# Four attention layers and a feed-forward on one core: last layer's weights kept as three values, smaller start loads, new instruction order

## The reference, cut to what matters

```
L0    post-norm cross attention, key mask        y = LN(x + Att(x, ctx) Wo + bo)
L1    the same, no mask                          y = LN(x + ...)
L2    pre-norm block: causal self attention (SELF), cross attention (CROSS), feed-forward 256-1024-256 (FFN)
L3    pre-norm cross attention with quantised weights:
      def bit_quant(W):
          gamma = mean(|W|)
          return clip(round(W / (gamma + 1e-5)), -1, 1) * gamma
      xn = layer_norm(x, ln_gamma, ln_beta)
      q = xn @ bit_quant(Wq).T + bq ;  k = ctx @ bit_quant(Wk).T + bk ;  v = ctx @ bit_quant(Wv).T + bv
      out = x + softmax(q k^T / 4) v @ bit_quant(Wo).T + bo
```

## Time and profile before

| | us |
|---|---|
| median of 3 runs | 1303.33 |
| the profiled execution, its own time | 1301.78 |
| its span, first to last instruction | 1299.9 |
| TensorE busy (union of matmuls) | 1240.0 |
| VectorE busy | 1065.7 |
| ScalarE busy | 793.9 |
| GpSimd busy | 706.1 |

### The profile page before, as it was taken

How to read it: one execution, slowest core, us unless ns; L and a number is a source line. 1 busy time by engine, 2 the same in 40 slices (tenths; PEclk the granted TensorE clock), 3 DMA queues, 4 the chain that set the end, 5 groups by cost and what they waited for, 6 DMA issues and landing times.

```text
span 1299.9 us, 42570 instructions
## 1 busy us (share of the span) xinstructions
PE 1240.0 (95%) x18540; PEld 1016.2 (78%) x18540; DVE 1065.7 (82%) x1826; ACT 793.9 (61%) x1263; POOL 706.1 (54%) x847
## 2 busy tenths in 40 slices
PE   7999999999999999999999999999999999899997
PEld 6777777777777788888888777777898989677775
DVE  6799998999999888798878999998544446888986
ACT  5666777757765676656658677666332424666654
POOL 5453667756885576364445246327856668324411
PEclk9999999999999999999999999999999999999999
DMA  6411101010110010000000001001010000001002
GB/s 240 126 38 30 45 10 34 9 34 17 28 31 3 2 34 11 3 2 3 2 3 3 12 16 34 25 19 38 5 33 1 1 1 2 9 10 34 26 3 99
DMA packets 16594, 34.89 MB, mean 27 GB/s; under 512 B 2071, under 2 KB 7447, under 8 KB 15895
## 3 DMA queue, kind: packets, MB, share of 16 engines
q1 hardware_dynamic: 16407, 32.16, 7.9%
HBM read 27.96 MB, written 4.19 MB: 25 GB/s over the span
## 4 chain that ended last, share of the span: by engine, by line
PE 55%; DVE 22%; POOL 10%; ACT 6%; issue 5%; DMA 2%; SPq 0%; POOLq 0%; DVEq 0%; ACTq 0%
DVE s_nm L1482 9%; PE ps L1111 7%; PE ps L996 6%; PE ps L1167 6%; PE ps L1179 5%; PE ps L1194 5%; PE ps L1148 5%; PE ps L1049 4%; PE ps L1008 3%; PE ps L1021 3%; ACT s_PU L1339 3%; DVE s_Os L1489 2%; DVE s_KH L1439 2%; PE ps L1126 2%; PE ps L1145 2%
## 5 line engine op out<-in xcount | busy, mean ns | idle before, releaser
L1482 DVE TENSOR_REDUCE s_nm<-ps 128x8 fp32r<-128x960 f32 (+1 forms) x352 | 398.1, 1160 | 40.2 <-PE ps L1049 19.0
L1339 ACT ACTIVATE s_PU<-ps 120x1024 f32<-120x1024 f32 (+1 forms) x288 | 281.9, 1023 | 110.6 <-PE ps L1126 109.6
L1667 POOL TENSOR_TENSOR s_Os<-s_Os,s_Rc 128x512 f32<-128x512 f32 x80 | 86.9, 1087 | 307.5 <-DVE s_Rc L1497 304.3
L1111 PE MATMUL ps<-s_Qs,s_KH 32*120 32x256 f32 (+2 forms) x4608 | 192.3, 289 | 13.3 <-DVE s_nm L1482 3.1
L1111 PEld LDWEIGHTS ps<-s_Qs,s_KH 32*120 32x120 f32 (+1 forms) x4608 | 154.6, 180 | 45.5 <-issue 13.0
L1167 PE MATMUL ps<-s_W,s_oT 128*128 128x256 f32 x960 | 134.5, 290 | 7.1 <-DVE s_oT L1411 6.2
L1148 PE MATMUL ps<-s_PU,s_Vp 120*32 120x256 f32 x2048 | 135.5, 388 | 4.2 <-DVE s_nm L1482 1.2
L996 PE MATMUL ps<-s_xT,s_W 128*128 128x256 f32 (+1 forms) x768 | 134.8, 324 | 3.3 <-DVE s_W L1416 1.0
L1167 PEld LDWEIGHTS ps<-s_W,s_oT 128*128 128x128 f32 x960 | 120.7, 191 | 16.4 <-issue 8.2
L1614 POOL TENSOR_TENSOR s_xs<-s_xs,s_rowv 128x512 f32<-128x512 f32 x96 | 125.2, 1304 | 11.4 <-POOL s_mv L1652 1.1
L1049 PE MATMUL ps<-s_KH,s_Qs 32*128 32x240 f32 x3072 | 126.9, 291 | 4.6 <-DVE s_nm L1482 2.4
(11 more groups left out here) (93 smaller groups left out, 2303.4 us busy)
## 6 DMA issues: line engine op xcount, KB each, us to landing
s_cf<-ctx_t SPq DMA_DIRECT2D x32, 240.0 KB, 2.7
s_ws<-weights SPq DMA_DIRECT2D x28, 256.0 KB, 2.9
s_nt<-x_t SPq DMA_DIRECT2D x16, 256.0 KB, 3.5
s_xs<-x_nat SPq DMA_DIRECT2D x4, 1024.0 KB, 7.5
out<-s_xs SPq DMA_DIRECT2D x16, 256.0 KB, 2.6
s_rowv<-rows SPq DMA_DIRECT2D x6, 512.0 KB, 3.8
s_mi<-mask SPq DMA_DIRECT2D x8, 120.0 KB, 4.2
s_who<-who SPq DMA_DIRECT2D x1, 128.0 KB, 3.5
```

Of the source, the lines that this page charges most:

```text
L1111: t = e.matmul(banks[j][0:n, wide * x:wide * x + wide], kz[row[j], lk, g, c, k0:k0 + n], q[row[j], lq, g, qs_], start=(x == 0 and y_ == 0) ...
L1339: t = e.activation(P_of(i, k)[0:n, :, :], pair("B", i, k)[0:n, :, :], ACT.Exp, scale=0.25)
L1482: e.tensor_reduce(o, v, AX.X, ALU.max, negate=True).then_inc(sem["max"])
L1667: e.tensor_tensor(o[:, :, 0:16], o[:, :, 0:16], rc.to_broadcast([128, 32, 16]), ALU.mult).then_inc(sem["pool"])
```

## The change

1. In L3 the weights hold -1, 0 and 1, which fp32r holds exactly, so the part with the rest of the weight falls away: `parts_of("L3")` is `PARTS[:2]`, 4 matmuls to an output tile in place of 6, in Q, K, V and O. The means are applied elsewhere: into x^T with the norm's scale (Th, Tl), and into the copies of K (K0), V (Ve) and O (y).
2. The making of these weights: qa keeps only its three small operations; qw is now two DVE operations of 128x512 straight into the weight's place, which wait until that place has been read last. Wh, Wl and wg of L3 are gone, and POOL's three operations.
3. Start: the constants are loaded sixth, `who` and `gone` much later (before SELF), the mask row goes to 4 partitions (the rest of the tile is set once by two memsets on DVE), x comes in eight loads of 512 KB.
4. The due times of all steps on all engines are new, and so are the planner's durations. By the two tables TensorE's list has 1213 steps in both, and changes between whole-array, row-tiled and column-tiled steps 660 times before and 661 times after.

```diff
+TERNARY = ("L3",)
-MOVED = dict(xT=.65, cT=.6, mi=.8, ws=.65, row=1.5, x=2.7, mci=.5, out=.65)
+MOVED = dict(xT=.65, cT=.6, mi=.15, ws=.65, row=1.5, x=1.35, msk=.6, cst=.4, mci=.4, out=.65)
-TURN = .19
+TURN = {("whole", "rows"): .195, ("columns", "rows"): .3, ("rows", "whole"): .185, ("columns", "whole"): .2,
+        ("whole", "columns"): .03, ("rows", "columns"): .03}
+def ready_of(layer, m):
+    return ("qw", m, 0) if layer in TERNARY else (rest_of(layer), layer, m)
+def parts_of(layer):
+    return PARTS[:2] if layer in TERNARY else PARTS
...
+        def mean_of(m): return gq[:, 4 * m + 1:4 * m + 2]
...   (in Q, K, V and O alike)
-                    for c, (cw, cx) in enumerate(PARTS):
+                    for c, (cw, cx) in enumerate(parts_of(layer)):
...   (Th on ACT, Tl on DVE)
+                    if layer_of(i) in TERNARY:
+                        w.wait_ge(sem["wa"], nth("wa", layer_of(i), 0))
+                        e.activation(to, half_of("T", i, f), ACT.Copy, scale=gg[:, f:f + 1]).then_inc(sem["Th"])
+                    e.scalar_tensor_tensor(xT_of(i)[:, 1, at, :], half_of("T", i, f), gg[:, f:f + 1], xT_of(i)[:, 0, at, :].bitcast(f32),
+                                           ALU.mult, ALU.subtract).then_inc(sem["Tl"])
...   (wa, K0, Ve, y)
+                    e.tensor_scalar(gg[:, :], c2[:, 20:22], mean_of(0), None, ALU.mult)
+                        t = e.activation(K0_of(i)[:, g, :], m[:, g * 256:g * 256 + n], ACT.Identity, bias=bk(layer_of(i), g), scale=mean_of(1))
+                        t = e.scalar_tensor_tensor(to, v, mean_of(2)[0:n], add, ALU.mult, ALU.add)
+                    e.scalar_tensor_tensor(to, bankM(name, i), mean_of(3), to, ALU.mult, ALU.add).then_inc(sem["y"])
...   (qa on DVE loses its last two operations, POOL loses qw; new on DVE:)
-                e.tensor_scalar(a1, w3(m), c[2], c[1], ALU.is_gt, ALU.mult)
-                e.tensor_scalar(b1, w3(m), c[3], c[1], ALU.is_lt, ALU.mult).then_inc(sem["qa"])
+            def qw(m):
+                over, under = (gq[:, 4 * m + k:4 * m + k + 1] for k in (2, 3))
+                to, low = (wv("L3", c, m).rearrange("p k n -> p (k n)") for c in range(2))
+                last = readers(*had_place("L3", m))
+                w.wait_ge(sem["qa"], 2 * nth("qa", m))
+                w.wait_ge(sem[last[0][0]], max(nth(*x) for x in last))
+                e.tensor_scalar(low, w3(m), under, None, ALU.is_lt).then_inc(sem["q1"])
+                w.wait_ge(sem["q1"], nth("qw", m))
+                e.scalar_tensor_tensor(to, w3(m), over, low.bitcast(f32), ALU.is_gt, ALU.subtract).then_inc(sem["qw"])
...   (start)
+                e.memset(mi[s][:, :], 1).then_inc(sem["cst"])
-            e.dma_start(cst[:, :], consts).then_inc(sem["d_cst"], 16)
-                e.dma_start(xs[:, 4 * n:4 * n + 4, :, :], x_nat[:, 4 * n:4 * n + 4, :, :]).then_inc(sem[f"d_x{n}"], 16)
+                e.dma_start(xs[:, 2 * n:2 * n + 2, :, :], x_nat[:, 2 * n:2 * n + 2, :, :]).then_inc(sem[f"d_x{n}"], 16)
-                e.dma_start(mi[slot("mi", i)][:, :], mask[i // 2].partition_broadcast(128)).then_inc(dma_ops["mi", i, 0][0], 16)
+                e.dma_start(mi[slot("mi", i)][0:128:32, :], mask[i // 2].partition_broadcast(4)).then_inc(dma_ops["mi", i, 0][0], 16)
+            def load_cst(i):
+                e.dma_start(cst[:, :], consts).then_inc(sem["d_cst"], 16)
```

More of the change, by code:

```diff
@@ L535, in step @@
                     cold = COLD
-                if array != ARRAY.get(name, "whole"):
-                    long += TURN
+                long += TURN.get((array, ARRAY.get(name, "whole")), 0.0)
                 array = ARRAY.get(name, "whole")
@@ L605, in make_plan @@
                     add("PE", "T", f, after=ready + ([("T", i, 0)] if f else []), rings=[("MI", ("T", i, f), [("Tl", i, f)])] + ([] if f else [("xT", i, users)]))
-                    add("ACT", "Th", f, after=[("T", i, f)])
+                    add("ACT", "Th", f, after=[("T", i, f)] + ([("wa", layer, 0)] if layer in TERNARY else []))
                     add("DVE", "Tl", f, after=[("Th", i, f)])
@@ L623, in make_plan @@
                 for g in parts:
-                    add("PE", "Q", g, long=1.33 if len(two) == 2 else None, after=x_t + [(rest_of(layer), layer, 0)] + ([("Q", i, 0)] if g else []),
+                    add("PE", "Q", g, long=.86 if layer == "L3" else 1.275 if len(two) == 2 else None, after=x_t + [ready_of(layer, 0)] + ([("Q", i, 0)] if g else []),
                         rings=[("MI", ("Q", i, g), [("Ql", i, g)])] + ([] if g else [("Q", x, [("B", x, u) for u in range(units(x))]) for x in two]))
@@ L637, in make_plan @@
                 behind = [("F1", 5 * B - 2, 7)] if layer == "L3" else []
-                add("PE", "K", after=ctx + [(rest_of(layer), layer, 1)] + behind, long=1.42 if self_ else None,
+                add("PE", "K", after=ctx + [ready_of(layer, 1)] + behind, long=1.42 if self_ else .9 if layer == "L3" else None,
                     rings=[("MI", ("K", i, 0), [("K0", i, 0)]), ("K0", i, [("Kl", i, 0)]),
@@ L643, in make_plan @@
                 add("DVE", "Kl", after=[("Kh", i, 0)])
-                add("PE", "V", after=ctx + [(rest_of(layer), layer, 2)],
+                add("PE", "V", long=.95 if layer == "L3" else None, after=ctx + [ready_of(layer, 2)],
                     rings=[("MI", ("V", i, 0), [("Ve", i, 0)]), ("Vp", i, [("PV", x, hf) for x in key_users(i) for hf in range(2)])])
@@ L650, in make_plan @@
                     + ([] if u else [("nm", i, [("M", i, 0)])]),
-                    long=1.05 if self_ else .79 if layer == "L0" else None)
+                    long=(.92 if u else 1.02) if self_ else .8 if layer == "L0" else None)
                 for q in range(2):
@@ L659, in make_plan @@
             for u in range(units(i)):
-                add("PE", "B", u, after=[("Ql", pair, g) for g in parts] + [("Kl", first, 0)], long=1.3 if u == 2 else None,
+                add("PE", "B", u, after=[("Ql", pair, g) for g in parts] + [("Kl", first, 0)], long=1.29 if u == 2 else None,
                     rings=[("S", ("B", i, 2 * u + q), [("exp", i, 2 * u + q)]) for q in range(2)]
                     + [("PU", ("P", i, 2 * u + q), [("PV", i, hf) for hf in range(2) if 2 * u + q in half_pairs(i, hf)]) for q in range(2)])
-                add("PE", "D", u, after=[("B", i, u), ("mTe", i, 0)], long=.44 if u == 2 else None)
+                add("PE", "D", u, after=[("B", i, u), ("mTe", i, 0)], long=.445 if u == 2 else None)
                 for q in range(2):
@@ L677, in make_plan @@
             add("DVE", "OTl", after=[("OTh", i, 0)])
-            add("PE", "O", after=[("OTl", i, 0), (rest_of(layer), layer, 3)], rings=[("MI", ("O", i, 0), [("y", i, 0)])])
+            add("PE", "O", long=.95 if layer == "L3" else None, after=[("OTl", i, 0), ready_of(layer, 3)], rings=[("MI", ("O", i, 0), [("y", i, 0)])])
             last = ("O", i, 0)
@@ L712, in make_plan @@
     p.add("SP", "mci", 0)
-    for k in range(4):
+    p.add("SP", "msk", 0)
+    p.add("SP", "cst", 0)
+    for k in range(8):
         p.add("SP", "x", k)
@@ L744, in make_plan @@
                 p.add("POOL", "Wl", layer, m, after=[("Wh", layer, m)])
-    p.add("DVE", "mc", 0, after=[("mci", 0, 0)])
+    p.add("DVE", "mc", 0, after=[("mci", 0, 0), ("cst", 0, 0)])
     for k in range(4):
         p.stages["exp", 0, k].after.append(("mc", 0, 0))
+    for i in range(2):
+        p.stages["Qh", i, 0].after.append(("cst", 0, 0))
+        p.stages["D", i, 0].after.append(("mc", 0, 0))
+    p.stages["K0", 0, 0].after.append(("cst", 0, 0))
+    for u in range(3):
+        p.stages["A", 2 * B, u].after.append(("msk", 0, 0))
     p.run()
@@ L884, in program @@
         for name, i, k in plan.order["POOL"]:
-            n_pool += len(both(i)) if name == "Xl" else {"bo": 1, "cap": 1, "rs": 4, "lng": 2, "Xl": 2, "Cl": 1, "Hl": 1, "nmul": 1, "Wl": 1, "qw": 3}[name]
+            n_pool += len(both(i)) if name == "Xl" else {"bo": 1, "cap": 1, "rs": 4, "lng": 2, "Xl": 2, "Cl": 1, "Hl": 1, "nmul": 1, "Wl": 1}[name]
             pool_ops[name, i, k] = n_pool
@@ L1424, in wa @@
                     o, add = fold_col(n, m), bankM("wb", n, m)[:, 0:2]
-                e.tensor_tensor(o, o, add, ALU.add).then_inc(sem["wa"])
+                if n in TERNARY:
+                    e.tensor_scalar(gg[:, :], c2[:, 20:22], mean_of(0), None, ALU.mult)
+                    e.scalar_tensor_tensor(o, add, mean_of(0), o, ALU.mult, ALU.add).then_inc(sem["wa"])
+                else:
+                    e.tensor_tensor(o, o, add, ALU.add).then_inc(sem["wa"])
             def Qlo(i, g0):
```

165 lines of the change are left out of this document (82 added, 83 removed), and 574 rows, old and new, of tables (AT, WANT).

## The result

The changed kernel takes 1291.21 us (median of 4 runs, 1289.46 to 1291.80) against 1303.68 of the kernel before on the same chip: ratio 0.9906, 95% interval 0.9885 to 0.9926. Forecast were 1281.5, range 1272 to 1291: the measured median lies 0.2 us outside. They ran on several chips, on which the kernel before took 1302.1 to 1303.3. With 4 to 12 runs of a kernel that scatter by 1 to 2 us each, a difference is known to about 2 us; what is smaller is called not measurable here.

What follows compares the result with a forecast made beforehand. In L3's body TensorE was taken to bind (95% busy), VectorE (88%) close behind. L3's gain 18, start 0.7 and order 2 sum to 20.7 us: 1301.78 to 1281.1 profiled, median 1281.5, range 1272 to 1291.

Steps and rivals of the forecast that it cites:

- L3's gain: L3 from its first K to the end, plus 0.9 us ahead: between 14 and 21 us less, 18 taken.
- The matmuls that go: L3's Q, K, V and O lose a part of three: 22.8 us less TensorE work, 21.9 behind the first K.
- What VectorE takes on: L3's copies Tl, Ve and y become scalar_tensor_tensor: 48 x 0.065 = 3.1 us more VectorE work, bounds 0 and 3.1.
- the lower bound: L3 if VectorE fills only to L1's 96%: 188.7 us against 202.1, 13.4 less, with the 0.9 in front 14.
- The making of the weights: In and ahead of the feed-forward: 0 us taken, 0 to 3 if qw's wait for the weight's place delays L3's start.
- The start: First loads of L0: less mask and constants ahead of the first x^T, 0.7 us less, bounds 0 and 1.2.
- The order: New lists can move every wait in L0, L1, SELF and CROSS: 2 us less taken, 8 kept both ways.
- VectorE as a wall: Rival, chance 0.18: L3 gives only 14 us, or 12 with the qw wait, the order nothing; 1287 us.
- The falling clock: Rival, chance 0.04: TensorE waits in short gaps, half-clock stretches cost at most 1.7 us each; sixteen in L3 give 1308.

Runs made afterwards that it cites:

- run with plain copies: Changed kernel with L3's Tl, Ve and y as tensor_tensor again in place of scalar_tensor_tensor, the means left out: 1291.58 us.
- spread kernel: Changed kernel with two sets of due times altered: qw of Wo later (1119.5) and L3's bias additions on POOL moved apart; 1287.21 us, ratio 0.9887.

## Why the prediction was wrong, step by step

**Sign and place were right**, the time was 9.7 us off, and the step that failed is the size of L3's gain: 18 us taken (0.9 of it ahead of L3's first K), 9.7 measured behind that K. In the profiled execution the sum was 20.7 and 12.3 came. Of the 8.4 missing, 7.4 are in L3 behind its first K, and 1.0 is the time outside the span, which I held fixed.

*The matmuls that go: right by their rows from start to start.* Eight matmuls of K take 1095.21 - 1094.23 = 0.98 us from start to start where twelve took 1.43, eight of V 0.94 where twelve took 1.51; Q's four took 1.03 ahead of M, a little more than 4 x 0.232.

*What VectorE takes on: right in size by the rows.* Tl takes 729 ns and y 733, as L1431's 736 had said and not L1405's 671 (the rule of the Trainium skill's "VectorE: DVE Perf Modes", section "The TRN2 errata", by which I had estimated 658 for both, is not borne out by them). Ve takes 464, was 415. That VectorE's busy time in L3 is 173.1, forecast 173.2, is partly luck: 3.2 of them are Wo's qw, which the forecast had at nothing, and 2.0 less are layer norm statistics that now lie ahead of the first K. The price of the longer copies is too small to be measured by the run with plain copies.

*L3's gain: the step that failed.* I bounded it by 14 and 21 and took 18, that is 185.0 us from first K to end, by the assumption that VectorE fills as in L1 (96%) or better. L3 took 192.4. There are two errors in it, about equal.

First, the lower bound itself missed: (173.2 - 6.4) / 0.96 + 14.9 = 188.7, and L3 took 192.4. Up to 1271.67 VectorE was busy 144.71 + 21.92 = 166.6 of 177.5 us, 93.9%. At 96% the body would be 1.8 us shorter and the 24.97 us behind it 2.1. The body lost it to the places shown above (2.00 us of TensorE's wait and a fall of the clock at 1186, 1.72 at 1098.94): with the bias additions spread and qw moved L3 took 188.8. That this is the bound's number is chance: VectorE's work had by then fallen to 167.6, for which the same rule gives 183.6, and its share ahead of the last 14.9 us was 93.2%. No kernel with the new operations and all of their work came to 96% in L3. The second stretch belongs to the drain already, as I read it: I let the drain begin with the last 14.93 us, and VectorE's share falls 25 us ahead of those. It did so in the kernel before, 21.23 of the 24.97 us from 1260.00, the difference of two of the earlier trace rows. In the spread kernel it falls too (21.32 of 25.00 us from 1245.80), so the collisions are not its cause; what is was not tried.

Second, I went 4 us above that bound, because POOL is less busy in L3 than in L1 and VectorE should so wait less for it. VectorE does hardly wait for POOL there (1.5 us in all ahead of turn). But POOL's two-input operations stretch VectorE's own, as 3.19 and 1.75 us against 1.33 and 0.69, and an idle POOL helps only if it is idle at the right time. This could have been seen before: Kl had 867 ns on average in L3 of the kernel before, too, and one of the sixteen took over twice the median (ns, min/median/max):

```profile
L1439 DVE SCALAR_TENSOR_TENSOR s_KH<-s_K,s_cst,s_KH x16: 617/712/1673, 1103.0 to 1258.5; 128x480 fp32r<-128x480 f32 x16
```

*The making of the weights: 0 taken, about 2.5 measured.* The range 0 to 3 held it by luck, the mechanism was another. I looked for the wait of qw on the weight's place. What came was the collision of qw with POOL's Hl, 2.76 us in place of 0.75, with Tl behind it.

*The start: 0.7 taken, 2.9 (masks alone) and 3.9 (masks and constants) measured* by undoing it, each to about 2 us. L0's first K moved by 0.7 (6.63 to 5.94). The bytes of the mask were the thing, as I had it, but I counted only what lies ahead of the first x^T, which is 1.0 of it; that the later mask loads carry the rest is not shown.

*The order: 2 taken, none to be seen ahead of L3.* The first K at 1094.2 looks like proof of 3.6 us and is not: in eleven profiled executions of kernels that are the same, or all but the same, up to there it stands at 1094.2 to 1097.9, mean 1095.9, 1.9 us less than in the one execution of before. The rows say where these 1.9 arise. The fifth K of L0, before and after:

```profile
101.75 1.50 PE L1008 MATMUL ps<-s_cT,s_W 128*128 128x240 f32 x11
```

```profile
98.62 1.61 PE L1035 MATMUL ps<-s_cT,s_W 128*128 128x240 f32 x12
```

In the eleven it stands at 99.9 on average, 1.8 less than before. From there to the first K of L3 it is 996.1 us before and 995.5 to 997.1, mean 995.9, in the eleven. So all of the gain ahead of L3 lies in the first 100 us, where the start's loads are, and so does most of the scatter. The 990 us behind them, in which every list is new and Q's 0.9 should show, gave 0.1. In the two kernels with the old order, the new operations and the small masks the first K of L3 stands at 1096.95 and 1096.02, hardly later. As a whole the new order is worth 10.1 us with the new operations, 3.5 to 5.2 of it the clock fall that it avoids. I had priced order and matmuls as terms that add. They don't: the kernel with all of the change but the order stands at 0.9994 of the kernel before (0.9950 with its clock fall filled), that with all but the fewer matmuls at 1.0017, and both together give 11 to 12 us. The smaller masks' 2.9 are in all of these.

*The rivals.* VectorE as a wall (1287) came nearest in time, but by luck: its mechanism would give nearly a microsecond for each microsecond of VectorE's work, and 2.0, 9.6 and 5.5 us less of it gave nothing, 1.7 and nothing. The falling clock took its part: 3.4 us long in L3 of the changed kernel, which can have cost 1.7 at most, and 13.7 in the old order, where it cost 3.5 (by the two traces) to 5.2 (by the medians). I held it to 1.7 us an instance, from stretches of 3.4; that one was four times as long.

## What to carry to other kernels

When one engine's work is cut and the next is at 88%, the gain is neither "all until the wall" nor "to the wall": here a microsecond of TensorE's was worth 0.57 and one of VectorE's at most 0.24, both as averages over cuts of 20 to 30 us. Read the drain as a stage of its own, and before trusting an engine's busy time look at the maximum of each group, not its mean: an operation that takes 0.68 in the median and once 1.75 names a collision, and moving what it collides with leaves nothing out (4.3 us here, seven due times). One execution's time of one event late in the program scattered by up to 3.7 us (1094.2 to 1097.9); a sum that matches it is no proof. To see what a stage gave, subtract an event at its start.
